# Ordering the operations of one step on VectorE and ScalarE: a drain between them, or a semaphore that the engine waits for itself

## The reference

```python
x = x + 0.5 * ffn(layernorm(x))
x = x + attn(layernorm(x))
x = x + 0.5 * ffn(layernorm(x))
```

```python
q = where(signatures > 0.3, 1, where(signatures < -0.3, -1, 0))
cluster_sigs = sign(q.reshape(8, 8, D).mean(axis=1))
cluster_idx = argmax(calibrate(xf @ cluster_sigs.T))       # piecewise linear, 8 knots
tile_idx = cluster_idx * 8 + argmax(calibrate(xf @ q.T) within the cluster)
comp = tanh(gelu(xf @ W1 + b1) @ W2 + b2)                  # 2 values per token
hh = relu(comp @ w1[tile_idx] + b1s[tile_idx])             # 16 per tile
mag = hh @ w2[tile_idx] + b2s[tile_idx]
y = layernorm(xf + mag * directions[tile_idx] * scale) * gamma + beta
```

## Time and profile before

| | us |
|---|---|
| median of 2 runs | 1369.23 (1365.62 to 1372.85) |
| the profiled execution | 1381.28 |
| its slowest core's span (core 5) | 1379.1 |
| PE / DVE / ACT busy on that core | 794.0 / 519.0 / 567.9 |

### The profile page before, as it was taken

How to read it: one execution, slowest core, us unless ns; L and a number is a source line. 1 busy time by engine, 2 the same in 40 slices (tenths; PEclk the granted TensorE clock), 3 DMA queues, 4 the chain that set the end, 5 groups by cost and what they waited for, 6 DMA issues and landing times.

```text
span 1379.1 us, 12131 instructions; the slowest of 8 cores (1352.8 to 1379.1 us)
## 1 busy us (share of the span) xinstructions
PE 794.0 (58%) x3458; PEld 301.7 (22%) x3458; DVE 519.0 (38%) x976; ACT 567.9 (41%) x560; POOL 13.7 (1%) x21
## 2 busy tenths in 40 slices
PE   2047651110999558888888888811599157651120
PEld 1033110000544212222222222200333033210000
DVE  0464817678300351110111111064622563706771
ACT  0052321221422458888888888812500052231220
POOL 1000000000000000000000000000000100000000
PEclk9999755555688657788878779865599558655555
DMA  7500000006000000000000000004000300000006
GB/s 192 94 1 0 0 0 0 0 0 92 1 0 0 0 1 1 1 1 1 1 1 0 1 1 1 1 9 52 1 1 0 34 1 0 0 0 0 0 0 243
DMA packets 23566, 25.45 MB, mean 18 GB/s; under 512 B 12874, under 2 KB 17227, under 8 KB 23506
## 3 DMA queue, kind: packets, MB, share of 16 engines
q0 software_dynamic: 12208, 7.09, 4.4%
q1 hardware_dynamic: 11298, 17.60, 4.0%
HBM read 23.39 MB, written 8.39 MB: 23 GB/s over the span
## 4 chain that ended last, share of the span: by engine, by line
PE 42%; DVE 22%; ACT 20%; issue 9%; DMA 3%; DVEq 1%; SPq 1%; ACTq 0%; POOL 0%; POOLq 0%
ACT sE L1224 10%; PE pQ L870 7%; PE pO L1008 5%; PE pTR L332 5%; DVE sSTAT L1224 5%; PE pS L1034 5%; PE pW L1171 5%; DVE sZ L1224 3%; DVE sYW L1224 3%; ACT sZ L1224 3%; PE pH L589 2%; ACT sHH L1224 2%; PE pM L662 2%; PE pS L642 2%; PE ptrA L1077 2%
## 5 line engine op out<-in xcount | busy, mean ns | idle before, releaser
L1224 ACT ACTIVATE sE<-pS,sNB 128x1024 bf16<-128x1024 f32 (+1 forms) x320 | 298.4, 994 | 30.0 <-PE pS L1034 26.1
L1008 PE MATMUL pO<-sE,sVTM 128*65 128x512 bf16 (+3 forms) x640 | 207.2, 413 | 8.8 <-DVE sE L1224 6.0
L332 PE MATMUL pTR<-sIDB,sXFB 128*128 128x128 bf16 x512 | 73.1, 256 | 123.3 <-ACT sXFB L1224 122.4
L1034 PE MATMUL pS<-sQT,sKT 64*128 64x512 bf16 (+3 forms) x640 | 127.3, 408 | 22.2 <-DVE sE L1224 14.2
L1224 DVE TENSOR_TENSOR sE<-sE,sTRI 128x256 bf16<-128x256 bf16 x128 | 37.4, 292 | 265.8 <-ACT sE L1224 265.5
L796 PE MATMUL pD<-sDIR,sWT 64*128 64x512 bf16 x64 | 31.9, 606 | 125.6 <-DVE sX L1224 123.7
L1224 ACT ACTIVATE sZ<-sYW,sRS 128x1024 bf16<-128x1024 f32 x32 | 39.7, 1242 | 139.1 <-DVE sYW L1224 139.1
L332 PEld LDWEIGHTS pTR<-sIDB,sXFB 128*128 128x128 bf16 x512 | 52.4, 102 | 145.1 <-issue 127.2
L1008 PEld LDWEIGHTS pO<-sE,sVTM 128*65 128x65 bf16 x640 | 49.5, 119 | 90.4 <-issue 83.7
L870 PE MATMUL pQ<-sT,sWQ 128*128 128x512 bf16 x256 | 65.9, 429 | 0.9 <-DVE sT L1224 0.9
L1034 PEld LDWEIGHTS pS<-sQT,sKT 64*128 64x128 bf16 x640 | 33.6, 95 | 150.1 <-issue 146.2
(11 more groups left out here) (162 smaller groups left out, 811.7 us busy)
## 6 DMA issues: line engine op xcount, KB each, us to landing
sX<-x SPq DMA_DIRECT2D x4, 2048.0 KB, 20.1
y<-sX SPq DMA_DIRECT2D x1, 8192.0 KB, 23.5
sWQ<-wq POOLq DMA_DIRECT2D x1, 2048.0 KB, 17.8
sWO<-wo POOLq DMA_DIRECT2D x1, 2048.0 KB, 17.2
sW1C<-cw POOLq DMA_DIRECT2D x2, 512.0 KB, 12.0
sSGR<-sigsT SPq DMA_DIRECT2D x2, 256.0 KB, 12.5
sWK<-wk POOLq DMA_DIRECT2D x1, 512.0 KB, 20.9
sWV<-wv POOLq DMA_DIRECT2D x1, 512.0 KB, 23.6
```

The costliest lines, as they stand in the source:

```text
L332: tt.transpose(pTR[:, par, c, :], sXFB[:, par, 128 * c:128 * (c + 1)], sIDB[:]),
L1008: mi = t.matmul(pO[:, h, lv:512], sVTM[:, c, gg, :], sE[:, epar, h, lv:512], start=(c == 0), stop=(c == cmax - 1))
L1034: mi = t.matmul(pS[:, cpar, h, lv:512], sKT[o:o + 64, kchunk, 128 * c:128 * (c + 1)], sQT[o:o + 64, hp, q0:qe], start=True, stop=True, til ...
L1224: return a(*args, **kw)
```

## The change

`DrainProxy` no longer issues `drain()`. It remembers the last operation that it issued in this step. When the next one comes, the last one gets an increment of a semaphore of its engine (`SD_v` or `SD_s`), the engine waits until the semaphore has reached the running count, and then the next operation is issued. The count runs on over all steps of the engine. Nothing else changes: the steps, their order, their other waits and marks are the same.

```diff
     class DrainProxy:
-        def __init__(self, eng):
+        def __init__(self, eng, sem, ctr):
             self._e = eng
-            self._n = 0
+            self._sem = sem
+            self._ctr = ctr
+            self._last = None
 
         def __getattr__(self, name):
             a = getattr(self._e, name)
             if name in OPS:
                 def wrapped(*args, **kw):
-                    if self._n > 0:
-                        self._e.drain()
-                    self._n += 1
-                    return a(*args, **kw)
+                    if self._last is not None:
+                        self._ctr[0] += 1
+                        self._last.then_inc(self._sem, 1)
+                        self._e.wait_ge(self._sem, self._ctr[0])
+                    self._last = a(*args, **kw)
+                    return self._last
                 return wrapped
             return a
 
+    for s in ("SD_v", "SD_s"):
+        P.new_sem(s)
+
     def run_for(eng_obj, tag):
         use_proxy = tag in ("v", "s")
+        ctr = [0]
         for stp in steps:
...
-                eo = DrainProxy(eng_obj) if use_proxy else eng_obj
+                eo = DrainProxy(eng_obj, sems["SD_" + tag], ctr) if use_proxy else eng_obj
```

## The result

| | before | after |
|---|---|---|
| median, us | 1368.32 (36 runs) | 1372.65 (37 runs) |
| ratio after / before | | 1.0034, 95% interval 1.0024 to 1.0044 |
| the profiled execution, us | 1381.28 | 1371.62 |
| core 5: span, us; granted clock | 1379.1; 0.715 | 1370.1; 0.732 |

The account below looks back on a forecast made before the run. No engine bounds the whole; the chain holds 42% of PE, 22% of DVE and 20% of ACT. 203 places on the path x 0.030 = 6.1 us, added to the median 1369.2, gave 1375.3 us; range 1367 to 1385.

Parts of the forecast that it names:

- The price: Between operations of one DVE step: a wait for itself 0.105 us against a drain's 0.075, so 0.030 us more each.
- the prediction's 18: Places on core 5, 78.19 to 1247.96 us, where DVE already waits for itself; gaps all 0.10 to 0.11 us.
- The count: 203 places on the path, 6.1 us; calibration, argmax and selection, 47 per block, hidden by idle time before sMGm.
- No cost at all: Rival at the 203 places: drain and semaphore hand-over cost the same; 1369.2 us; chance 0.07.
- The clock: Rival: granted clock, 5.9 us between the feed-forward stages, carries the result to or below the time before; chance 0.14.
- Early waits: Rival at the 203 places: wait passed earlier than the drain, gap below 0.075 us, at most -30.5 us; chance 0.03.
- Dear waits: Rival at the 203 places: waits cost as in rows of several, 19.3 us up to 33.5 us; chance 0.06.
- The upper bound: Price from above: behind barriers, where DVE passes several waits, gaps of 0.17 to 0.24 us, +0.095 to +0.165.
- my mechanism: Between DVE operations: semaphore's value arrives about 0.03 us after the operation's end, by its own way, while a drain runs.
- The last 14 statistics operations: Unguarded DVE operations, said to start 8.39 / 14 = 0.60 us apart and last 0.674 each, so they overlap.
- the lower bound: Price from below: overlap as without drain or wait, gap of -0.075, -0.15 us per place; held nearly excluded.
- The 23 waits in a row: Argument for dear waits: up to 23 waits follow each other among operations of 0.18 us.

Follow-up runs that it names:

- e1: Kernel before, with the semaphore form only in calibration, argmax and selection (94 places), drains elsewhere; ratio 1.0002 (0.9989 to 1.0015).
- e2: Kernel before, with the semaphore form everywhere but calibration, argmax and selection (213 places), drains there; ratio 1.0053 (1.0039 to 1.0067).
- e3: Kernel before, drains kept, each operation ahead of one also increments the semaphore, nobody waits; ratio 1.0041 (1.0026 to 1.0057).
- e12: Kernel before, with a long-met wait for a setup load behind each drain, no increments; ratio 1.0099 (1.0073 to 1.0125).
- e6: Against the kernel before: semaphore form with each wait issued twice in place of the drain; ratio 1.0141 (1.0125 to 1.0156).
- e4: Against the kernel before: increment, drain, then wait in every place; ratio 1.0124 (1.0106 to 1.0142).
- e7: Kernel before, with independent operations of a step grouped and only the first guarded by a drain; 1359.76 us, ratio 0.9932.
- e9: Kernel before, with a long-met wait for a setup load ahead of each drain, no increments; ratio 1.0012 (0.9991 to 1.0034).
- e8: e7 with the tail reordered, next tile's sYW before this tile's gamma and beta; against the kernel before, 1312.03 us, ratio 0.9579.
- e5: Kernel before, with two drains in each place instead of one; ratio 1.0068 (1.0050 to 1.0086).
- e10: Against the kernel before: increment, wait, then drain in every place; ratio 1.0119 (1.0085 to 1.0153).
- e11: Kernel before, with four drains in each place instead of one; ratio 1.0242 (1.0177 to 1.0307).

## Why the prediction was right

**The price.** It was read from waits that the kernel before already had between its steps, 0.105 us, against drains of 0.075. Its packed trace has 20 places on core 5 with a single wait for DVE's own mark: 19 with gaps of 0.103 to 0.107 us, in each of which the increment is recorded 10 to 12 ns after the operation's end and the wait's record starts 38 or 39 ns after it, and one of 0.150 us ahead of a memset, 925.45 to 925.60 us, which the prediction's 18 leave out. The changed kernel has 0.103 and 0.108. The difference of 0.030 came out as 0.028 on the yardstick, and as 0.029 in the medians of all places. This step carried the forecast, and it held although I had no true idea of what the price is made of.

**The count.** 203 places on the path and 94 hidden in the two selections: e1 and e2 show it from both sides, and the table above shows it for ten forms. With 0.028 the computed loss is 5.7 us, inside the measured 3.3 to 6.0, if near its upper end. That the changed kernel lies somewhat below (4.7 us) and e2 somewhat above (7.3 us) may be scatter; it is not settled.

**The rivals.** No cost at all falls with the interval 1.0024 to 1.0044 and with the gaps. Both parts of the new form have a price of their own: an increment ahead of a drain costs 0.016 us (e3), and a wait behind one 0.069 (e12). Early waits fall: none of the change's 305 gaps on DVE lies below 0.10 us (the least is 0.102). The clock gave and took in single executions. The changed kernel's windows for the two feed-forward stages, to be set beside 169.90 and 175.80 in the earlier trace rows:

```profile
60.20:238.25 178.05, 92.12 (x395) 41.72 (x396) 95.73 (x197) 49.19 (x35) 0.00 (x0) 0.73 0.00 1
1082.98:1255.61 172.63, 86.41 (x395) 40.17 (x396) 95.61 (x197) 49.19 (x35) 0.00 (x0) 0.64 0.00 1
```

The first stage is 8.2 us longer than before, at 0.73 where it was 0.77, though its 50 places on the path account for 1.5 us only; the second is 3.2 us shorter, at 0.64 where it was 0.62. Over many runs no such difference was left. Dear waits: they exist, but for the second wait in a row, which adds 0.069 us (e6), not for the first, with which the gap is 0.028 over the drain's.

**Where it was off.** The upper bound rested on a wrong reading. I took the barriers' 0.17 to 0.24 us as what one wait might cost in the worst case. The records show two waits inside the gap of 0.17 us and three inside that of 0.24 (the others of the row are passed beside the operation before), so these are 0.104 plus once and twice the 0.069 of e6. And my mechanism, stated before e3 and e4 and left vague in the prediction, fell as I had stated it: it gave the increment nothing, and e3 shows 0.016 us; it gave a wait behind a drain at most 0.125 us in all, and e4 shows 0.159. A wait whose value has long arrived (e12) already costs 0.069 us, more than the 0.047 of a second drain, so no late value is needed to make it the dearer one. What fills the 27 ns between the increment and the record of the change's wait, the value's way or the queue itself, stays open. In sums of the gaps, the wait costs 0.012 us more than the drain when both have the increment (0.103 against 0.091), and the increment makes up the rest.

Three remarks of the prediction were loose, without effect on the sum. The last 14 statistics operations have 13 steps, so they start (8.39 - 0.674) / 13 = 0.594 us apart, and the lower bound is 0.08 + 0.075 = 0.155 us per place. The 23 waits in a row stand in the calibration, among operations of up to 1.4 us, not of 0.18. And the waits' gaps of 0.10 to 0.11 us are not under a tenth of a microsecond.

## What to carry to other kernels

To price a synchronisation that is to replace another, look in the trace for places where the kernel already has the new form with the same neighbours, measure the gaps in both, and count the places off the hidden chains; that gave 6.1 us where 4.7 were measured. What paid here was not the form of the guard but its absence: group operations that are independent (about 0.15 us each, e7), have nothing stand between the guard and the next operation (a met wait there cost 0.069 us, e12), and put a wait that is sure to be met ahead of the guard, where the gap stayed at 0.075 us (e9). And compare with the large idle rows first: the 1.44 us for ACT per tile were worth 46 to 48 us, by a change of order (e8 against e7), and all guards on the path together hold 203 x 0.075 = 15 us.

## What the runs showed of the hardware that I had not expected

- An increment that nobody waits for lengthens the gap behind a drain from 0.075 to 0.091 us (e3).
- A wait in DVE's queue whose value is there already costs 0.069 us behind a drain or another wait (e12, e6), and nothing ahead of the drain (e9).
- A drain behind another drain or behind a wait costs 0.040 to 0.047 us (e5, e10, e11).
- In front of the tail's last additions, the next operation starts 44 to 46 ns after the record of its last guard ends, whether that is a drain or a wait (before, after, e3 to e6, e9 to e12).
